# Attention block: who adds which head's probabilities, when context pieces are split, and how the last softmax inverse is made

## What is computed

```python
q, k, v = proj(wq, bq), proj(wk, bk), proj(wv, bv)       # 16 heads of 32
probs = softmax(q @ k.T / sqrt(32), axis=-1)
ctx = probs @ v
x = layernorm(x + ctx @ wo.T + bo)
x = layernorm(x + routed_experts(x) + sigmoid(x @ se_gate_w.T) * shared_expert(x))
```

## Time and profile before

| what | us |
|---|---|
| three runs | 2120.12, 2120.41, 2124.7 (median 2120.41) |
| profiled execution | 2123.44, its span 2121.7 |
| busy in the span: PE, VectorE, ScalarE, GpSimd | 2021.2, 1288.4, 878.8, 875.2 |
| VectorE busy in the window 900 to 940 | 31.05 of 40 |
| L953, VectorE's addition, by buffers: shortest, median, longest | 0.68, 0.95 to 0.98, 2.60 |
| L924, one maximum: median | 0.68 (back to back they start about 0.62 apart) |

### The profile page before, as it was taken

The page is one execution under the profiler, slowest core; times in us unless marked ns, Lnnn a source line. Parts: engine busy times, 40 slices in busy tenths (PEclk is TensorE's granted clock), DMA queues, the critical chain, the costliest instruction groups (busy, mean ns, idle before and its releaser), DMA issues. The chain is left out here.

```text
span 2121.7 us, 30279 instructions
## 1 busy us (share of the span) xinstructions
PE 2021.2 (95%) x9764; PEld 1225.0 (58%) x9765; DVE 1288.4 (61%) x2279; ACT 878.8 (41%) x1562; POOL 875.2 (41%) x830
## 2 busy tenths in 40 slices
PE   7999999999999999999999975899999999999997
PEld 5655556655556655556655434578544444446886
DVE  6777776777776677776778843574222222225875
ACT  2366664466664466663566562321111111112332
POOL 3255654556654556653555543400111111114651
PEclk9999999999999999999999998899999999999999
DMA  7321434231434231335132204652222222225752
GB/s 228 70 61 46 101 76 114 106 76 36 96 76 135 86 79 43 94 68 164 56 76 48 74 12 153 217 231 62 88 89 89 89 89 89 89 79 159 228 175 75
DMA packets 96449, 213.27 MB, mean 101 GB/s; under 512 B 24704, under 2 KB 25216, under 8 KB 93120
## 3 DMA queue, kind: packets, MB, share of 16 engines
q1 hardware_dynamic: 85520, 176.24, 28.0%
q0 software_dynamic: 10800, 35.40, 6.1%
HBM read 118.77 MB, written 41.94 MB: 76 GB/s over the span
## 5 line engine op out<-in xcount | busy, mean ns | idle before, releaser
L924 DVE TENSOR_REDUCE max_half<-ps_side 128x1 f32<-128x512 f32 x1024 | 658.1, 682 | 200.1 <-PE ps_side L651 197.1
L651 PE MATMUL ps_side<-kq_stack 96*128 96x512 f32 x1024 | 408.6, 403 | 4.9 <-DVE max_half L924 2.3
L673 PE MATMUL ps_s<-kq_stack 97*128 97x512 f32 x937 | 393.6, 421 | 10.4 <-ACT probs_first L826 5.6
L673 PEld LDWEIGHTS ps_s<-kq_stack 97*128 97x128 f32 x937 | 177.6, 190 | 170.7 <-issue 85.5
L1600 PE MATMUL ps_gu<-gu_sb,xT_e 128*128 x568 | 257.7, 596 | 0.7 <-issue 0.5
L1498 POOL DMA_INDIRECT x_g<-x,who_all x71 | 67.3, 948 | 455.0 <-PE ps_t L1590 353.4
L826 ACT ACTIVATE probs_first<-ps_s 128x512 f32<-128x512 f32 x326 | 187.5, 599 | 109.1 <-PE ps_s L673 93.8
L651 PEld LDWEIGHTS ps_side<-kq_stack 96*128 96x128 f32 x1024 | 194.7, 190 | 57.9 <-DVE max_half L924 26.5
L826 ACT ACTIVATE probs_mid<-ps_s 128x512 f32<-128x512 f32 x308 | 177.6, 599 | 114.1 <-PE ps_s L673 99.6
L581 POOL TENSOR_TENSOR acc<-probs_first,probs_mid 128x512 f32<-128x512 f32 x129 | 163.3, 1292 | 147.4 <-ACT probs_mid L826 147.4
L581 POOL TENSOR_TENSOR acc<-probs_last,probs_first 128x512 f32<-128x512 f32 x129 | 162.8, 1288 | 132.4 <-ACT probs_first L826 132.4
(11 more groups left out here) (233 smaller groups left out, 3329.2 us busy)
## 6 DMA issues: line engine op xcount, KB each, us to landing
kq_stack<-kq SPq DMA_DIRECT2D x192, 256.0 KB, 5.1
y_slots<-y_t SPq DMA_DIRECT2D x71, 256.0 KB, 2.3
res<-inv_rows SPq DMA_DIRECT2D x128, 64.0 KB, 2.0
x_r<-x SPq DMA_DIRECT2D x32, 256.0 KB, 3.9
x_t<-x SPq DMA_DIRECT2D x32, 256.0 KB
gu_sb<-wgu SPq DMA_DIRECT2D x8, 1024.0 KB, 15.6
out<-gu_sb SPq DMA_DIRECT2D x32, 256.0 KB, 2.7
stage<-wkqT SPq DMA_DIRECT2D x28, 256.0 KB, 3.0
```

Of the source, the lines that this page charges most:

```text
L651: nc.tensor.matmul(bank, q_stack[par][0:3 * HD, h, t * P:(t + 1) * P], k_stack[par][0:3 * HD, h, half * HALF:(half + 1) * HALF], start=Tru ...
L673: nc.tensor.matmul(out, k_stack[par][0:3 * HD + 1, h, kt * P:(kt + 1) * P], q_stack[par][0:3 * HD + 1, h, half * HALF:(half + 1) * HALF], ...
L924: nc.vector.reduce_max(max_half[:, u // 2, u % 2:u % 2 + 1], bank, AX.X).then_inc(side_free, 1)
```

## The change

- **Addition.** VectorE adds head 0, GpSimd heads 1 to 3 (in the last group of the last batch VectorE 0 and 1, GpSimd 2 and 3). VectorE's place is behind slot 0 instead of slot 1 of the odd step.
- **GpSimd waits.** Where more GpSimd work stands behind an addition (normalising, splitting, low parts of x), it first waits for VectorE's addition.
- **Context pieces.** In the last group ScalarE converts one piece behind each odd step 1 to 13, VectorE subtracts one behind each even step 2 to 14.
- **x.** ScalarE converts chunks behind the same steps as GpSimd subtracts them (`X_AFTER`).
- **Last inverse.** VectorE inverts the copied sums where they are, 128x256 twice, with no DMAs; GpSimd multiplies, ScalarE and VectorE split the two halves separately. Output tiles 4 and 5 need the first, 6 and 7 the second.

```diff
-CTX_HIGH_LAST = {10: (0, 1, 2), 12: (3, 4, 5), 14: (6,)}
+CTX_HIGH_LAST = {1 + 2 * i: i for i in range(7)}
+CTX_LOW_LAST = {2 + 2 * i: i for i in range(7)}
-X_HIGH = {(1, 8): (0, 1), (2, 0): (2,), (2, 1): (3,), (2, 4): (4,), (2, 5): (5,), (2, 7): (6,), (2, 8): (7,)}
 X_AFTER = {(1, 9): (0, 1), (2, 1): (2, 3), (2, 5): (4, 5), (2, 7): (6,), (2, 9): (7,)}
...
+        PARTS_LAST = [slice(i * HALF // 2, (i + 1) * HALF // 2) for i in range(2)]
+        def dve_heads(b, loc):
+            return HG - pool_heads(b, loc)
...
-                few((b + 1) * G * NHALF - 1)
+                if not last:
+                    few((b + 1) * G * NHALF - 1)
...
-                invert((b + 1) * G * NHALF - 1)
-                sp.wait_ge(ctx_done, (b + 1) * G * NHALF)
+                if not last:
+                    invert((b + 1) * G * NHALF - 1)
+                sp.wait_ge(ctx_done, INVERSES + 1 if last else (b + 1) * G * NHALF)
...
+            def normalise_last(part):
+                out = ctx_sb[:, G - 1, HALF + PARTS_LAST[part].start:HALF + PARTS_LAST[part].stop]
+                pool.wait_ge(inverted, INVERSES + part)
+                nc.gpsimd.tensor_tensor(out, out, rinv[:, PARTS_LAST[part]], ALU.mult).then_inc(ctx_done, 1)
-                i = loc // FOLD
-                for h in range(pool_heads(b, loc)):
+                i, first = loc // FOLD, dve_heads(b, loc)
+                for h in range(first, HG):
...
                         fold(b, loc)
+                        if (g, at) in X_AFTER or at in (*NORM_AFTER, NORM_AFTER_LAST, SPLIT_W_AFTER):
+                            pool.wait_ge(folded_dve, added_dve(b, loc // FOLD + 1))
...
+                if last:
+                    for part in range(2):
+                        normalise_last(part)
                 add_bo(b, 0)
                 add_bo(b, 1)
-                normalise(b, G - 1, 1)
+                if not last:
+                    normalise(b, G - 1, 1)
...
+                if t == KT - 2 and isinstance(b, int) and b == B - 1:
+                    pe.wait_ge(part_low, C + INVERSES + 1)
...
-                    for i in X_HIGH.get((g, loc % STEPS), ()) if not last else ():
+                    for i in X_AFTER.get((g, loc % STEPS), ()) if not last else ():
                         x_part(b + 1, i)
-                    for i in CTX_HIGH_LAST.get(loc % STEPS, ()) if last and g == G - 1 else ():
-                        ctx_high(b, i)
+                    if last and g == G - 1 and loc % STEPS in CTX_HIGH_LAST:
+                        ctx_high(b, CTX_HIGH_LAST[loc % STEPS])
-            ctx_high(B - 1, CTX_PARTS - 1)
+            for part in range(2):
+                ctx_high_last(part)
...
+            def invert_last(part):
+                if part == 0:
+                    dve.wait_ge(sum_taken, INVERSES)
+                    dve.wait_ge(ctx_done, INVERSES - 1)
+                nc.vector.reciprocal(rinv[:, PARTS_LAST[part]], rsum[:, PARTS_LAST[part]]).then_inc(inverted, 1)
-                i, first = loc // FOLD, pool_heads(b, loc)
-                for h in range(first, HG):
+                i, first = loc // FOLD, 0
+                for h in range(dve_heads(b, loc)):
-                        if slot == 1 and loc % FOLD:
+                        if slot == 0 and loc % FOLD:
                             fold(b, loc)
-            invert((b + 1) * G * NHALF - 1)
+            for part in range(2):
+                invert_last(part)
             for t in range(KT):
                 o_tile(b * TAIL + KT + t, b, t, tail_bank(t))
-                if t == 1:
-                    ctx_low(b, CTX_PARTS - 1)
+                if t < 2:
+                    ctx_low_last(t)
```

More of the change, by code:

```diff
@@ L967, in batch @@
                                 invert(k if half == 0 else k - NHALF, half == 0 and g == 0)
-                    for i in CTX_HIGH_LAST.get(loc % STEPS, ()) if last and g == G - 1 else ():
-                        ctx_low(b, i)
+                    if last and g == G - 1 and loc % STEPS in CTX_LOW_LAST:
+                        ctx_low(b, CTX_LOW_LAST[loc % STEPS])
             def ctx_low(b, i):
```

20 lines of the change are left out of this document (15 added, 5 removed).

## The result

| | before | after |
|---|---|---|
| median of the runs on one chip (4 each), us | 2122.43 (2120.12 to 2124.7) | 2100.44 (2098.37 to 2103.5) |
| ratio, 95% interval | | 0.9898 [0.9879, 0.9916] |
| profiled execution / its span | 2123.44 / 2121.7 | 2100.07 / 2098.3 |
| granted clock of TensorE over the span | 0.989 | 0.988 |

The account below looks back on a forecast made before the run. TensorE was taken as busy nearly throughout attention, idling at three places: last group, last tail, waits for VectorE's addition. Gains 2.7 + 1.7 + 7.2 + 8.4 = 20.0 us gave 2103.4 from the profiled execution, 2100.4 from the median; range 2094 to 2112.

Parts of the forecast that it names:

- Last group: Last head group of the last batch: single context pieces hide, eight pairs take 48.5 instead of 55.7 us; gain 7.2.
- The 0.1 a pair for the swap: Last group: with heads swapped GpSimd's addition waits for VectorE's two, so a pair takes 6.0 instead of 5.88 us.
- Tail: Last output projection: without the inverse's DMAs PE's wait and slow clock go, 26.5 instead of 34.9 us; gain 8.4.
- Additions in ordinary groups: The 15 groups before the last: PE's 6.2 us of waits for VectorE's addition go, less charges; net gain 2.7.
- The charge of 0.2 for each eighth pair: A group's eighth pair of steps, without projection beside it: PE's sums wait 0.2 us, 3.0 us over 15 pairs.
- x conversions: ScalarE's conversions moved behind odd steps: one PE wait of 0.56 us goes in each of three batches; gain 1.7 us.
- ordinary groups give nothing: Rival for the ordinary groups: eighth-pair waits of 0.6 and later additions eat the 4.4 us; 2107.8 us, chance 0.18.
- VectorE as the bound: Rival for pairs with projections: VectorE's additions lose turns to GpSimd and delay PE; 22 us slower, 2142, chance 0.07.
- A slow tail: Rival for the tail: slow reciprocal or collision keeps part of PE's wait; gain 5.5, 2103.3 us; chance within forecast's 0.70.
- a last group at 6.5 a pair: Rival for the last group: GpSimd begins with head 2, 52 us, gain 3.7, 2103.9 us; chance within forecast's 0.70.

Follow-up runs that it names:

- pieces alone: Kernel before with only the last group's context pieces converted and subtracted one at a time: 2121.7 us, 3.8 less by the ratio 0.9982; last group 49.01 us.
- slot 1 again: Changed kernel with VectorE's addition moved back behind slot 1 of the odd step: one execution, 2111.14 us, last group 48.82 us.
- the wait alone: Kernel before with only GpSimd's wait for VectorE's addition ahead of its other work, heads and slots unchanged: one execution, 2119.01 us.
- one-piece kernel: Changed kernel with the last half inverted, multiplied and split in one piece of 512 columns: one execution, 2098.51 us, tail 26.78 us.
- heads, slot and wait: Kernel before with only the head swap, VectorE's addition behind slot 0 and GpSimd's wait: 2125.23 against 2124.93 us, ratio 1.0001.
- after's second profile: The changed kernel, unaltered, run once more on another kernel's chip: 2103.39 us, ratio to before 0.9910.

## Why the prediction was right, and where its terms were not

The time and the sign came out as forecast: 2100.44 against 2100.4. Two terms were right within 0.8 us, the ordinary groups gave more than twice what I had put down, and a loss that I didn't forecast covered part of it.

- **Last group** (forecast 7.2, measured 7.95). The mechanism held in its parts: heaps 6.7 (pieces alone), and 1.3 in the fifth pair, of which the inverse's place is 1.1 (slot 1 again) and the rest goes with the swap and the wait. First pair 6.53 (6.5 forecast). The 0.1 a pair for the swap was wrong: the pairs stayed at 5.88. I had let GpSimd's first addition wait for VectorE's two, to 1229.1; in after it takes 0.13 more than two undisturbed ones (2.65 against 2.52), since VectorE's are nearly done when head 2 comes.
- **Tail** (8.4, measured 8.14). Each step came within 0.4 us: reciprocals 1.7 a half (1.76 by the slope, 1.9 taken), bias at T+5.9 (T+6.3), output tile 0 on VectorE at T+7.3 (T+7.6), low part T+10.0 (T+10.1), fifth tile T+12.0 (T+12.0), end T+26.8 (T+26.5). The Trainium skill's eight repeats ("VectorE: DVE Perf Modes", First, the fixed hardware budget), an estimated 2.1 us, are above the measured 1.7; the straight line through the earlier trace rows was nearer.
- **Additions in ordinary groups** (+2.7 net, measured +4.3 without the x conversions' part, the fifth pair of batch 3 and the rest: 5.7 gained, 1.4 lost). The gain was right: five long pairs go from 8.08 to 6.84, and 6.2 us with them, less the charge. The charge of 0.2 for each eighth pair was twice too large; it is 0.10 (6.84 to 6.94). GpSimd's end has 0.05 of room, and VectorE's turn falls between. The two short pairs cost 0.3 each, 0.6 where 0.5 stood. Not counted was 0.84 in batch 3, where an inverse made the addition late and the normalisation took its turn; the wait alone removes it.
- **x conversions** (1.7, measured 4.3). This is the step that failed: "The others are moved likewise and waited for by nobody now". Two more places in each batch cost 0.3 us, and the named one costs 0.83, not the 0.56 that stands in brackets at 505.27. The idle before one matmul is only that matmul's; the delay of the pair is read from the distance between two row sums. The experiment with this edit alone shows the same three places, in eight of the nine pairs.
- **Not forecast**: the transitions, +5.1 in this profile, the first sum +1.0 and the expert part -2.8, +3.3 together. Against the profiled execution the forecast was 2103.4 and 2100.07 came: 6.2 more from the ordinary groups, 0.7 from the last, 0.3 less from the tail, 3.3 given back. The medians agree to 0.1 us since the fresh runs of before lie 2 us above those I started from. That is luck, and so is part of the agreement to some 3 us with the profiled execution: it has these four errors of both signs in it.

**The rivals.** That ordinary groups give nothing is refuted by the rows (-10.6), though not by the whole time of this edit alone (1.0001), where the gain doesn't come through. VectorE as the bound: refuted, PE waits 1.6 us for maxima as before, and VectorE's additions in after have a median of 0.82 to 0.83, under the 0.95 to 0.98 of before. The Trainium skill's rule that VectorE and GpSimd shut each other out for an instruction ("SBUF — State Buffer", SBUF: two separate sides) agrees with the rows shown here (1.80 and 2.60 us beside GpSimd, 0.67 and 0.68 alone); but amid GpSimd's three additions VectorE got its turn at the next boundary (the longest of its additions in after is 1.60 us), and the place where it lost a further turn was behind them, before a normalisation. A slow tail and a last group at 6.5 a pair didn't happen.

**Open.** The 3 us in the first transition. Timeline of after, SyncE's queue and PE:

```profile
343.72 0.33 SPq L426 DMA_DIRECT2D wv_lo<-wv_lo_kept  x1
...
354.03 0.77 PE L635 MATMUL ps_side<-wv_hi,x_hi 128*128 128x512 f32 x1 [3.27 <-issue]
```

PE starts the projection of v 10.3 us after the load of `wv_lo` was issued; that it waits for this load is read from the order, since the trace names no releaser. In the one-piece kernel, which is the same program up to here, the load is issued at 343.23 and PE starts at 350.64 with no such wait. So the change doesn't bring it for certain. Of the seven profiles with swapped heads six have it (1.7 to 3.35 us), of the six with the heads as before two (x conversions 2.0, wait 1.8). Five of the seven have a first transition of 60.3 to 60.9 us, none of the six one over 58.5. That speaks for the swap making it likelier, by a way that nothing here shows; it isn't settled. It may also be what hides the gain of heads, slot and wait in their whole time.

## What to carry to other kernels

When two engines share a way and one has more work queued, make it wait for the other's short operation, or issue that one earlier; don't leave the turn to chance. In a stage bound by elementwise work, ask which engine does it faster and stands idle: one number in the code was worth 7 us here. Read the cost of a delay from the distance between two fixed events of the loop, not from the idle time of one row, and look for every place with the same pattern as the one found.

## What the runs showed of the hardware

- **The turn is not first come, first served.** An addition that VectorE had issued 0.8 us before GpSimd finished was sometimes passed by GpSimd's next operation and sometimes not, at places with the same code: in 5, 4, 4 and 1 of 14 places in the four profiles with VectorE's addition on head 3 behind slot 1 and no wait, in none with the wait.
- **Reciprocal.** 0.252 us for 16 columns, 0.353 for 32, 1.7 for 256 (half of 3.37 for two), 3.35 for 512: 5.9 to 6.5 ns for each further column.
- **The clock after an idle.** In after, PE idles 1.83 us until 1018.57 and then runs at the lower of the two levels for some matmuls: the granted clock is 0.64 from 1018.5 to 1023.2 and 1.00 in the 4.8 us behind. Rows of PE in that timeline:

```profile
1018.57 0.50 PE L691 MATMUL ps_s<-kq_stack 97*128 97x512 f32 x1 [1.83 <-ACT probs_first L846]
...
1019.18 0.63 PE L738 MATMUL ps_side<-wo_hi,ctx_lo 128*128 128x512 f32 x1
```

  Such matmuls take 0.39 to 0.40 elsewhere; seven in a row are slow here, 0.43 apart instead of 0.23, some 1.5 us in all. In after's second profile the same idle of 1.83 us was followed by none (granted clock 1.00 over the same 4.7 us). The third transition took 59.15 in the one and 57.72 in the other. It isn't evenly spread over the kernels, though: of the seven profiles of after and the kernels made from it six have such matmuls here (third transition 58.6 to 59.4), of the six others none (56.9 to 57.9). What tips it isn't known.
- **Code that nobody edits moves.** The expert part took 809.0 to 816.6 us over the 13 profiles. A part under 4 us can't be judged by the whole time of one kernel; its own rows can.
